# Householder reduction of a 256x256 matrix: the next column from the reflected product, scalars during the products, first product on x alone

## The reference

```python
d_inv_sqrt = jnp.where(deg > 0, jax.lax.rsqrt(deg), 0.0)
L = jnp.diag(deg) - A
L_norm = d_inv_sqrt[:, None] * L * d_inv_sqrt[None, :]
_, U = jnp.linalg.eigh(L_norm)
agg = jnp.einsum('mn,bnd->bmd', U.T, features)
h = jax.nn.relu(agg @ W1 + b1)
out = h @ W2 + b2
return jnp.einsum('nm,bmd->bnd', U, out)
```

## Time and profile before

| | us |
|---|---|
| three runs, median (lowest to highest) | 7619.89 (7603.49 to 7624.76) |
| profiled execution, its time | 7623.76 |
| its span in the trace | 7622.0 |
| the stage `tridiagonalise`, 42 to 1437 of the span | 1395 |

### The profile page before, as it was taken

The page is one execution under the profiler, slowest core; times in us unless marked ns, Lnnn a source line. Parts: engine busy times, 40 slices in busy tenths (PEclk is TensorE's granted clock), DMA queues, the critical chain, the costliest instruction groups (busy, mean ns, idle before and its releaser), DMA issues. The chain is left out here.

```text
span 7622.0 us, 81119 instructions
## 1 busy us (share of the span) xinstructions
PE 4954.3 (65%) x22112; PEld 3479.5 (46%) x22112; DVE 4404.4 (58%) x17933; ACT 1555.7 (20%) x3409; POOL 852.4 (11%) x653
## 2 busy tenths in 40 slices
PE   5666544332003799740079967777697997977999
PEld 5666433210002577520069933333376443646676
DVE  5555666798995333348988866666633223343332
ACT  1111111243001244420000000000043532442333
POOL 0000000001000000000000068888400000000000
PEclk9999999975556799865555578888798997888799
DMA  0000000000000000010000000000000000000000
GB/s 24 1 1 1 1 1 1 1 1 1 1 1 1 12 0 0 2 12 21 0 0 0 0 4 4 4 4 4 3 0 13 0 0 7 0 3 12 1 0 22
DMA packets 72449, 30.60 MB, mean 4 GB/s; under 512 B 46714, under 2 KB 67860, under 8 KB 71956
## 3 DMA queue, kind: packets, MB, share of 16 engines
q1 hardware_dynamic: 52756, 23.65, 1.4%
q0 software_dynamic: 19456, 4.40, 0.9%
HBM read 22.89 MB, written 5.11 MB: 4 GB/s over the span
## 5 line engine op out<-in xcount | busy, mean ns | idle before, releaser
L1274 PE MATMUL l1f_ga_acc<-l1f_gas_prod,l1f_gas_ohl 128*128 128x512 f32 (+1 forms) x1824 | 778.8, 580 | 261.8 <-DVE l1f_gas_prod L1233 174.2
L1161 PE MATMUL l1f_gap_hist<-l1f_gap_ohh,l1f_gap_ohl 128*128 128x64 bf16 x4096 | 539.9, 308 | 361.4 <-DVE l1f_gap_ohh L1145 360.6
L1161 PEld LDWEIGHTS l1f_gap_hist<-l1f_gap_ohh,l1f_gap_ohl 128*128 128x128 bf16 x4096 | 492.8, 149 | 408.4 <-DVE l1f_gap_ohh L1145 400.7
L1274 PEld LDWEIGHTS l1f_ga_acc<-l1f_gas_prod,l1f_gas_ohl 128*128 128x128 f32 x1824 | 359.0, 208 | 681.7 <-issue 425.1
L1249 POOL DMA_INDIRECT l1f_gas_rs<-l1f_ga_table_s,l1f_gas_sidx x304 | 405.6, 1334 | 1016.0 <-DVE l1f_gas_didx L1205 923.6
L1683 PE MATMUL l0g_tri_dots<-l0g_tri_Z 128*128 128x7 f32 (+31 forms) x762 | 208.1, 394 | 462.2 <-DVE l0g_tri_Z L1850 448.5
L1233 DVE TENSOR_TENSOR l1f_gas_prod<-l1f_gas_ohh,l1f_gas_msg 128x1280 f32<-128x1280 f32 x304 | 454.2, 1494 | 10.4
L1249 POOL DMA_INDIRECT l1f_gas_rd<-l1f_ga_table_d,l1f_gas_didx x304 | 416.7, 1371 | 101.5 <-issue 101.5
L1260 ACT ACTIVATE l1f_gas_ex<-l1f_gas_ex 128x32 f32<-128x32 f32 x38 | 8.7, 229 | 2003.8 <-DVEq L1214 1896.2
L1683 PEld LDWEIGHTS l0g_tri_dots<-l0g_tri_Z 128*128 128x128 f32 x762 | 181.4, 318 | 479.6 <-DVE l0g_tri_Z L1848 462.5
L1143 DVE TENSOR_TENSOR l1f_gap_ohl<-l1f_gap_rep,l1f_gae_dlow 128x2048 bf16<-128x2048 bf16 x256 | 314.0, 1226 | 73.1 <-PE l1f_gap_hist L1161 72.6
(11 more groups left out here) (842 smaller groups left out, 10054.4 us busy)
## 6 DMA issues: line engine op xcount, KB each, us to landing
l1f_gas_rs<-l1f_ga_table_s,l1f_gas_sidx POOLq DMA_INDIRECT x304
l1f_gas_rd<-l1f_ga_table_d,l1f_gas_didx POOLq DMA_INDIRECT x304
out_dram<-top_x SPq DMA_DIRECT2D x2, 2048.0 KB, 12.2
l1f_gae_src<-in_L_ffn_edge_index_dram SPq DMA_DIRECT2D x1, 2048.0 KB, 7.3
l1f_gae_dst<-in_L_ffn_edge_index_dram SPq DMA_DIRECT2D x1, 2048.0 KB, 11.8
l2f_w<-in_L_ffn_expert_w_dram SPq DMA_DIRECT2D x3, 384.0 KB
l0f_l0f_W<-in_L_ffn_W_dram SPq DMA_DIRECT2D x1, 1024.0 KB
l1f_l1f_W<-in_L_ffn_W_dram SPq DMA_DIRECT2D x2, 512.0 KB
```

What stands on the lines that cost most here:

```text
L1161: last = nc.tensor.matmul(hist[:, :], ohl[:, j, :, c], ohh[:, j, :, c], start=False, stop=False)
L1274: last = nc.tensor.matmul(acc[:, c0 * T:c1 * T], ohl[:, c % 2, :], prod[:, c % 2, c0:c1, :].rearrange("p c t -> p (c t)"), start=False, st ...
```

## The change

The next column is taken in another way. Before, y (from `ya[.., 1]`, NB, `ya[.., 0]`) went into base and two values of late into a factor g. After, base is KV times As times x below the diagonal, and the factor of the vector `vm` is the first value of late alone; the scalars for it (`den`, `nk`, `KV`, `knk`) no longer pass through t1, t2, t3, g1, g and kb. A column whose norm is nearly zero is handled by a flag kept for each column (`ZF`), by `still` in base, and by `moved`, which zeroes such columns when the vectors are kept.

On TensorE the first product matmul stands ahead of the wait for w and of the dots; the late product waits for `ya_set` and `v_set`, which the instructions that write ya and v raise themselves. On VectorE `c1` and KK come after the instruction for x. In the first half `ya` is made after `vm`, in the second ahead of `den`. ScalarE makes nkh first and yn when `y_set` is up; yn is subtracted in w instead of added. The copies of the vectors go from ScalarE to three VectorE instructions (`keep_vectors`), placed at a strip's end between `swapped` and the wait for rank, and once after the loop. In the excerpt twelve columns of indentation are cut, and the declarations are left out.

```diff
         pe.wait_ge(x_set, i + 1)
-        pe.wait_ge(w_set, i)
         if J == 0 and i > 0:
             pe.wait_ge(applied, strip_of(i))
+        nc.tensor.matmul(prod[:, hs[0]:hs[0] + 1], As[:, hs[0], bass.ts(hs[0], P)], Z[:, b, hs[0], 0:1], start=True,
+                         stop=(hs[0] == 1))
+        pe.wait_ge(w_set, i)
         for h in hs:
             last = nc.tensor.matmul(dots[:, 0:1 + 2 * J], Z[:, b, h, 0:1].to_broadcast([P, P]), Z[:, b, h, 0:1 + 2 * J],
                                     start=(h == hs[0]), stop=(h == 1))
         last.then_inc(dots_done, 1)
-        nc.tensor.matmul(own[:, 0:1 + 2 * J], eye[:, h1, r:r + 1].to_broadcast([P, P]), Z[:, b, h1, 0:1 + 2 * J],
-                         start=True, stop=True).then_inc(own_done, 1)
-        for m in hs:
+        last = nc.tensor.matmul(own[:, 0:1 + 2 * J], eye[:, h1, r:r + 1].to_broadcast([P, P]), Z[:, b, h1, 0:1 + 2 * J],
+                                start=True, stop=True)
+        last.then_inc(own_done, 1)
+        if hs == (0, 1):
+            nc.tensor.matmul(prod[:, 0:1], As[:, 1, 0:P], Z[:, b, 1, 0:1], start=False, stop=True)
             for h in hs:
-                last = nc.tensor.matmul(prod[:, m:m + 1], As[:, h, bass.ts(m, P)], Z[:, b, h, 0:1],
-                                        start=(h == hs[0]), stop=(h == 1))
-        last.then_inc(prod_done, 1)
-        pe.wait_ge(late_in, i + 1)
+                last = nc.tensor.matmul(prod[:, 1:2], As[:, h, P:N], Z[:, b, h, 0:1], start=(h == 0), stop=(h == 1))
+            last.then_inc(prod_done, 1)
+        pe.wait_ge(ya_set, i + 1)
+        pe.wait_ge(v_set, i + 1)
...
         act.wait_ge(nk_set, i + 1)
+        nc.scalar.activation(w["nkh"], w["nk"], ACT.Square, scale=0.5 ** 0.5).then_inc(act_step, 1)
+        act.wait_ge(y_set, i + 1)
         nc.scalar.activation(yn[:, h0:], y[:, h0:], ACT.Copy, scale=w["nk"]).then_inc(act_step, 1)
-        nc.scalar.activation(w["nkh"], w["nk"], ACT.Square, scale=0.5 ** 0.5).then_inc(act_step, 1)
         act.wait_ge(w_set, i + 1)
         nc.scalar.activation(VA[:, i:i + 1], late[:, 1:2], ACT.Copy).then_inc(va_kept, 1)
         J, k = i % STRIP, strip_of(i)
-        if J == STRIP - 1 or i == LAST - 1:
-            top = min(i + 1, P - 1) - k * STRIP
-            if top > 0:
-                nc.scalar.activation(VV[:, 0, k * STRIP:k * STRIP + top], Z[:, k % 2, 0, 1:2 * top:2], ACT.Copy)
-            nc.scalar.activation(VV[:, 1, k * STRIP:i + 1], Z[:, k % 2, 1, 1:2 + 2 * J:2], ACT.Copy).then_inc(kept, 1)
...
+    def keep_vectors(i, k, b):
+        n = i + 1 - k * STRIP
+        link(ts(moved[:, 0:n], ZF[:, k * STRIP:i + 1], -1.0, 1.0, ALU.mult, ALU.add))
+        for h, top in ((0, min(n, P - 1 - k * STRIP)), (1, n)):
+            if top > 0:
+                link.free(tt(VV[:, h, k * STRIP:k * STRIP + top], Z[:, b, h, 1:2 * top:2], moved[:, 0:top], ALU.mult))
+        dve.wait_ge(dve_step, link.n)
+    def current_times_x(i, J, h0, r, corr_at):
+        if h0 == 0:
+            dve.wait_ge(prod_done, i + 1)
+        if J > 0:
+            dve.wait_ge(dve_step, corr_at)
+            ins = tt(ya[:, h0:, r, 0], prod[:, h0:HALF], corr[:, h0:], ALU.add)
+        else:
+            ins = nc.vector.tensor_copy(ya[:, h0:, r, 0], prod[:, h0:HALF])
+        ins.then_inc(ya_set, 1)
...
+        link.free(ts(ZF[:, at], dots[:, 0:1], 1e-30, None, ALU.is_lt))
+        zf_at = link.n
         dve.wait_ge(own_done, i + 1)
         link.free(ts(w["sgn"], own[:, 0:1], 0.0, 2.0, ALU.is_ge, ALU.mult))
         sgn_at = link.n
-        link.free(ts(w["al2"], own[:, 0:1], 2.0, None, ALU.mult))
...
         dve.wait_ge(dve_step, sgn_at)
-        link(stt(NB[:, at], w["sgn"], -1.0, w["root"], ALU.add, ALU.mult))
-        link.free(stt(v, eye[:, h0:, r], NB[:, at], x, ALU.mult, ALU.add))
-        v_at = link.n
-        link.free(tt(w["t1"], w["al2"], NB[:, at], ALU.add))
+        link.free(stt(w["ax"], w["sgn"], -1.0, own[:, 0:1], ALU.add, ALU.mult))
+        link.free(stt(w["ns"], ZF[:, at], 1e30, dots[:, 0:1], ALU.mult, ALU.add))
+        ns_at = link.n
+        link.free(stt(NB[:, at], w["sgn"], -1.0, w["root"], ALU.add, ALU.mult))
+        nb_at = link.n
+        if h0 == 1:
+            current_times_x(i, J, h0, r, corr_at)
+        dve.wait_ge(dve_step, ns_at)
+        link.free(ts(w["den"], w["root"], w["ax"], w["ns"], ALU.mult, ALU.add))
+        den_at = link.n
+        dve.wait_ge(dve_step, nb_at)
+        stt(v, eye[:, h0:, r], NB[:, at], x, ALU.mult, ALU.add).then_inc(v_set, 1)
         link.free(tt(V1[:, at], own[:, 0:1], NB[:, at], ALU.add))
-        dve.wait_ge(prod_done, i + 1)
-        if J > 0:
-            dve.wait_ge(dve_step, corr_at)
-            link.free(tt(ya[:, h0:, r, 0], prod[:, h0:HALF], corr[:, h0:], ALU.add))
-        else:
-            link.free(nc.vector.tensor_copy(ya[:, h0:, r, 0], prod[:, h0:HALF]))
-        dve.wait_ge(dve_step, link.n)
-        dve.sem_inc(late_in, 1)
-        link(stt(w["t2"], w["t1"], NB[:, at], dots[:, 0:1], ALU.mult, ALU.add))
-        link.free(stt(y[:, h0:], ya[:, h0:, r, 1], NB[:, at], ya[:, h0:, r, 0], ALU.mult, ALU.add))
-        y_at = link.n
-        link.free(ts(w["t3"], w["t2"], 1e-30, -0.5, ALU.max, ALU.mult))
-        dve.wait_ge(dve_step, link.n)
+        v1_at = link.n
+        dve.wait_ge(dve_step, den_at)
         if i > 0:
             dve.wait_ge(act_step, 2 * i)
-        link(nc.vector.reciprocal(w["nk"], w["t3"]))
-        dve.sem_inc(nk_set, 1)
-        link.free(tt(KV[:, at], w["nk"], V1[:, at], ALU.mult))
+        nc.vector.reciprocal(w["nk"], w["den"]).then_inc(nk_set, 1)
+        link.free(stt(still[:, h0:], ya[:, h0:, r, 1], ZF[:, at], below[:, h0:, r], ALU.mult, ALU.mult))
+        still_at = link.n
+        dve.wait_ge(nk_set, i + 1)
+        dve.wait_ge(dve_step, v1_at)
+        link.free(stt(KV[:, at], w["nk"], -1.0, V1[:, at], ALU.mult, ALU.mult))
         kv_at = link.n
-        link.free(stt(vnm[:, h0:], v, w["nk"], below[:, h0:, r], ALU.mult, ALU.mult))
+        if h0 == 0:
+            dve.wait_ge(dve_step, kv_at)
+            link.free(stt(w["knk"], KV[:, at], -1.0, w["nk"], ALU.mult, ALU.mult))
+            dve.wait_ge(dve_step, link.n)
+            dve.wait_ge(v_set, i + 1)
+            link.free(stt(vm[:, h0:], v, w["knk"], below[:, h0:, r], ALU.mult, ALU.mult))
+            current_times_x(i, J, h0, r, corr_at)
+        dve.wait_ge(ya_set, i + 1)
+        stt(y[:, h0:], ya[:, h0:, r, 1], NB[:, at], ya[:, h0:, r, 0], ALU.mult, ALU.add).then_inc(y_set, 1)
         dve.wait_ge(dve_step, kv_at)
-        link.free(stt(base[:, h0:], y[:, h0:], KV[:, at], ya[:, h0:, r, 1], ALU.mult, ALU.add))
+        link.free(stt(base[:, h0:], ya[:, h0:, r, 0], KV[:, at], below[:, h0:, r], ALU.mult, ALU.mult))
         base_at = link.n
-        link.free(ts(w["kb"], KV[:, at], NB[:, at], 1.0, ALU.mult, ALU.add))
+        if h0 == 1:
+            link.free(stt(w["knk"], KV[:, at], -1.0, w["nk"], ALU.mult, ALU.mult))
+            dve.wait_ge(dve_step, link.n)
+            dve.wait_ge(v_set, i + 1)
+            link.free(stt(vm[:, h0:], v, w["knk"], below[:, h0:, r], ALU.mult, ALU.mult))
         dve.wait_ge(dve_step, base_at)
-        link.free(tt(base[:, h0:], base[:, h0:], below[:, h0:, r], ALU.mult))
+        link.free(tt(base[:, h0:], base[:, h0:], still[:, h0:], ALU.add))
         dve.wait_ge(dve_step, link.n)
         dve.wait_ge(late_done, i + 1)
-        link.free(tt(w["g1"], late[:, 1:2], w["kb"], ALU.mult))
-        g1_at = link.n
+        if J == STRIP - 1 and k > 0:
+            dve.wait_ge(turned_done, k)
+        stt(Z[:, nb_next, h0:, 0], vm[:, h0:], late[:, 0:1], base[:, h0:], ALU.mult, ALU.add).then_inc(x_set, 1)
         link.free(tt(w["c1"], late[:, 1:2], NB[:, at], ALU.mult))
-        c1_at = link.n
-        dve.wait_ge(dve_step, g1_at)
-        link.free(stt(w["g"], late[:, 0:1], KV[:, at], w["g1"], ALU.mult, ALU.add))
-        g_at = link.n
-        dve.wait_ge(dve_step, c1_at)
+        dve.wait_ge(dve_step, link.n)
         dve.wait_ge(act_step, 2 * (i + 1))
         link.free(ts(KK[:, at], late[:, 0:1], w["c1"], w["nkh"], ALU.add, ALU.mult))
-        kk_at = link.n
-        dve.wait_ge(dve_step, g_at)
-        if J == STRIP - 1 and k > 0:
-            dve.wait_ge(kept, k)
-            dve.wait_ge(turned_done, k)
-        stt(Z[:, nb_next, h0:, 0], vnm[:, h0:], w["g"], base[:, h0:], ALU.mult, ALU.add).then_inc(x_set, 1)
-        dve.wait_ge(dve_step, kk_at)
-        stt(wv, v, KK[:, at], yn[:, h0:], ALU.mult, ALU.add).then_inc(w_set, 1)
+        dve.wait_ge(dve_step, link.n)
+        stt(wv, v, KK[:, at], yn[:, h0:], ALU.mult, ALU.subtract).then_inc(w_set, 1)
...
             dve.sem_inc(swapped, 1)
+            keep_vectors(i, k, b)
             dve.wait_ge(rank_done, k + 1)
...
+    keep_vectors(LAST - 1, strip_of(LAST - 1), strip_of(LAST - 1) % 2)
```

17 lines of the change are left out of this document (10 added, 7 removed).

## The result

Four runs of the changed kernel have a median of 7480.95 us (7463.90 to 7500.92), beside 7617.19 us for the kernel before (7603.49 to 7624.76): a ratio of 0.9824, 95% interval 0.9800 to 0.9848. The profiled execution has a span of 7462.2 us, at the low end of its runs.

What follows compares the result with a forecast made beforehand. One serial loop per column bounds the tridiagonal stage, with TensorE's product late in the first part and VectorE's single-value chain setting the second half. Terms -49-95+4=-140 us from the median 7619.9 give 7480 us, range 7440 to 7535.

Steps and rivals of the forecast that it cites:

- w later: c1, KK behind x (T: x's start; S: first VectorE step after the root) make S 0.42 us later a column.
- First product: On TensorE, two product instructions run between x and w, end by about T+0.85, delay nothing; products end about S+1.4.
- rival D: Loop not shortened: the early product holds the dots back by its whole 0.46 us; 7597 us; chance 0.04.
- First half: Scalars at 54 old columns: ya now behind VectorE, x at S+3.52 (before 4.22), period 5.74 us against 6.02.
- Rival B: First half gains nothing, its bare scalar chain 0.38 us longer than counted, period stays 6.02; 7529 us; chance 0.12.
- Fewer old columns: First half: strips average 15.5 old columns, not 27: -0.13 us, bubbles +0.03; mean period 5.64, -49 us in all.
- Rival E: Handover and products overlap better, first half ends at 5.5 us a column; 7460 to 7445 us; chance 0.08.
- Second half: S to x 2.19 us instead of 3.36, period 3.97 against 4.72: -95 us; two signal instructions, 0.12 each, go.
- ScalarE: yn is there at S+2.9 or 2.0, KK needs it at S+3.8 or 2.5: hidden.
- strip ends: Seven: first product after `applied`, ahead of the dots, +0.43 us each, 3 us; keeping vectors hidden, the last bare 0.7 us.
- A scalar from PSUM: Scalar operand late in x, read from PSUM, not in the trace: 0 to 0.06 us a column, 15 us; taken as 0.
- Rival F: A PSUM operand costs a VectorE step its interval twice: ZF, ax, ns 0.2 us a column; 7530 us; chance 0.05.

Runs made afterwards that it cites:

- e1: Changed kernel with all product matmuls put back behind the dots and own: 7497.70 us, ratio 0.9839, stage 1253 us against 1241.
- e3: Changed kernel with products behind dots and own, and c1 and KK ahead of x: 7415.78 us, ratio 0.9754, stage 1195 us.
- e9: e3 with one TensorE wait ahead of the dots (x for the first column, w for all others): 7408.43 us, ratio 0.9738, stage 1181 us.
- e6: Kernel before with the first product matmul ahead of the wait for w and the dots: 7606.01 us, ratio 0.9990.
- e5: Kernel before with ya, v and the reciprocal raising their semaphores themselves, its own algebra kept: 7528.03 us, ratio 0.9890, stage 1298 us.
- e4: Changed kernel with the signals after ya and the reciprocal again in instructions of their own: 7581.50 us, ratio 0.9953, stage 1345 us.
- e7: Changed kernel with four more already met VectorE waits a column (ahead of ax, v, base, base's sum): 7471.00 us, ratio 0.9817.
- e11: Changed kernel with first-half ya right after still; second half c1 and KK ahead of x, product behind own, one wait, c1 ahead of vm: 7365.51 us.

## Why the prediction was right

The mechanism is the one forecast: in the two columns read above, the steps came within 0.05 us of the sum. That the median lies 1 us from 7480 is partly luck. The sum was for the stage, -140, and the stage moved by -147 in the profiles (1388 to 1241), while the medians moved by 136 and the untouched rest varies by more than that difference.

1. *w later:* KK at T+0.33 and w at T+0.64 (forecast 0.31, 0.62), the dots' handover (w's end to the start of their weights) 0.06 instead of 0.04; S at T+2.26 and 1.82 instead of 2.22 and 1.78. The price of two waits instead of one, 0.07, was right, and e1, e3 and e9 show it (0.05 to 0.07). Among its signs the prediction has w "0.49 after x"; by its own sum 0.49 is what is added to 0.13, and 0.62 is the place.
2. *First product:* it hides in the wait for w and adds nothing: the sum gave it no gain, and e1 and e6 bear that out. It had no room to spare. The working (from T+0.25, 0.46 long) gives T+0.71, the text says T+0.85, and it ends at T+0.86, as w does (384.58). That it holds nothing back is shown by the handover from w, 0.06 with it and in e9 without it, so rival D is out. The title of the change names it; on its own it earns nothing in this kernel.
3. *First half:* S to x 3.47 for 3.52. The one term that was off is the blocked second wait: late's end to x is 383.72-383.61=0.11, where 0.03+0.12=0.15 was counted. From x to S 0.04 too little was counted (0.02 up to KK and w, 0.02 in the handover), and the two nearly cancel: period 5.73 for 5.74. Rival B, no gain in this half, is out.
4. *Fewer old columns:* the period runs from 5.44 with one old column to 5.73 with 27, 0.011 for each, as forecast. A bubble is a step that starts late without a wait to explain it. Bubbles were fewer than allowed for and larger: 16 of 123 columns, 0.22 on average, where one in four at 0.14 was counted; both make 0.03 a column. By the rows of x the first half took 51 us less, for 49 forecast (0.38 by 127 is 48). Rival E, 5.5 a column, is not reached: the mean of the plain columns is 5.63.
5. *Second half:* S to x 2.17 for 2.19, period 3.99 for 3.97; 96 us less by the rows of x, for 95 forecast. But the reason given was unevenly split: the two signal instructions stood for 0.12 each. The one after ya cost 0.18 (e5) to 0.25 (e4), since VectorE's next steps did not need ya at all and were stopped for the whole of its write. The sum itself has the short step (ya 0.68, den 0.75), so only the explanation falls short. e4 and e5 put the signals at 91 to 104 us of stage, against the 61 us that 2 x 0.12 x 254 gives.
6. *ScalarE* and the strip ends: KK never waited for yn. Strip ends were forecast 0.43 longer on top of a plain column. A column that starts a strip has few old columns, so the plain one to take off is that with one (medians of each half). In the first half that gives 10.88-5.44=5.44 after and 11.39-6.03=5.36 before, 0.1 more; in the second 7.03-3.87=3.16 and 7.42-4.61=2.81, 0.35 more. For seven that is under 2 us where 3 were counted.
7. *A scalar from PSUM:* the form that the trace of before didn't have:

```profile
L1872 DVE SCALAR_TENSOR_TENSOR l0g_tri_Z<-l0g_tri_vm,l0g_tri_late,l0g_tri_base x254: 223/226/228, 46.9 to 1288.1; 128x2 f32<-128x2 f32 x64, 128x1 f32<-128x1 f32 x63
```

It takes 226 ns (223 to 228), where the earlier trace rows has 0.21 for L1848. With a start-to-start of 0.14 (383.72 to 383.86) instead of 0.13 it costs 0.01 a column, 3 us; the value taken was 0, the bound 15.

Rival F is out as well: ZF starts 0.07 ahead of sgn (380.51 to 380.58) though it reads PSUM. The Trainium skill's "Perfetto Trace Analysis", section Optimizing Scalar/DVE Operations, has about 125 ns on PSUM against 60 on SBUF; this trace does not agree for steps of one value, which start 0.07 apart on either.

## What to carry to other kernels

Where a chain of single-value steps sets the time, write down each step's start from the one before (0.07, 0.13 or 0.19 us here, by the number of scalars in memory, and 0.03 past the write where it is needed) and who waits for whom; the sum hit each step of the two columns that were read within 0.05 us. Let the instruction that makes a value raise the semaphore itself: a wait and a signal of its own stop everything behind them in the queue. Work moved into a gap earns nothing unless it was what the next step waited for: ask that of each part by itself, and of pairs, since two edits that each cost 12 to 14 us of stage alone took 46 off it together (e3).

## What the runs showed of the hardware

- A wait for a write and a signal in instructions of their own, where the next step doesn't need that write, cost 0.25 us (ya to den 0.32 in e4, 0.07 in the changed kernel).
- A further wait that is met in time costs nearly nothing on VectorE (e7, four a column, 4 us in all). A wait that stands in an instruction of its own ahead of a step and is the last to be met costs some 0.06 on TensorE (w's end to the weights 0.11 in e1, 0.06 in e9) and 0.07 on VectorE (late's end to x 0.107, late's end to c1 0.038 in e11, where it is the only wait; medians of 127 columns).
- In every kernel here one column in 6 to 14 is 0.1 to 0.5 us longer, mostly without a wait that the profile names. e7, with four more waits a column, has the most (40 of 246, against 26 in the changed kernel). What makes these bubbles wasn't tried.
